# A scan kernel whose background work is moved to other chunks: new positions on four engines, and C's rows 56 bytes further on

## The reference, cut to what matters

```python
xz = x @ in_w.T + in_b
xm, res = jnp.split(xz, 2, axis=-1)
xc = conv_general_dilated(xm, conv_w)             # 4 taps, each channel by itself
xm = silu(xc + conv_b)
x_dbl = xm @ xp_w.T
delta = softplus(x_dbl[..., :64] @ dt_w.T + dt_b)
Bm, Cm = x_dbl[..., 64:80], x_dbl[..., 80:96]
A = -exp(A_log)

def step(h, ins):                                  # 512 channels x 16 states
    d_t, B_t, C_t, u_t = ins
    h = h * exp(d_t[:, :, None] * A) + (d_t * u_t)[:, :, None] * B_t[:, None, :]
    return h, einsum('bds,bs->bd', h, C_t)

y = (ys + xm * D_ssm) * silu(res)
return y @ out_w.T + out_b
```

## Time and profile before

| | us |
|---|---|
| median of 3 runs | 3793.13 (3785.04 to 3797.67) |
| profiled execution | 3805.45 |
| its span | 3804.0 |

### The profile page before, as it was taken

How to read it: one execution, slowest core, us unless ns; L and a number is a source line. 1 busy time by engine, 2 the same in 40 slices (tenths; PEclk the granted TensorE clock), 3 DMA queues, 4 the chain that set the end, 5 groups by cost and what they waited for, 6 DMA issues and landing times.

```text
span 3804.0 us, 45601 instructions
## 1 busy us (share of the span) xinstructions
PE 2862.1 (75%) x15274; PEld 2092.5 (55%) x15275; DVE 2344.1 (62%) x3190; ACT 1933.3 (51%) x3239; POOL 1890.0 (50%) x1807
## 2 busy tenths in 40 slices
PE   3787777787787987777777777777988179999930
PEld 2666556566565554565555665565565146666620
DVE  4877778778784434787777787785333123333338
ACT  4776777776673324767766867764223011111100
POOL 2777677677685010687766777776110510100042
PEclk8888999999899987889998999999998589999975
DMA  5010011011012010001100111111002111311022
GB/s 212 29 33 30 29 31 32 29 32 37 32 43 65 1 34 23 23 31 30 33 29 26 34 31 34 33 41 39 26 23 92 68 46 61 116 62 60 32 65 80
DMA packets 100973, 171.52 MB, mean 45 GB/s; under 512 B 14514, under 2 KB 52658, under 8 KB 100786
## 3 DMA queue, kind: packets, MB, share of 16 engines
q1 hardware_dynamic: 82066, 119.38, 9.9%
q0 software_dynamic: 15392, 47.99, 3.4%
q10 hardware_dynamic: 3328, 1.76, 0.2%
HBM read 126.75 MB, written 42.34 MB: 44 GB/s over the span
## 4 chain that ended last, share of the span: by engine, by line
PE 49%; DVE 21%; issue 12%; ACT 8%; POOL 8%; DMA 2%; SPq 0%; another core or an unknown queue 0%; DVEq 0%; POOLq 0%; ACTq 0%
PE psD L1056 16%; PE psD L1378 6%; PE psD L1152 6%; DVE arena L1580 6%; POOL arena L703 6%; PE psA L1172 4%; DVE arena L1528 3%; DVE arena L1561 2%; PE psD L1121 2%; PE psD L1255 2%; PE psA L1056 2%; PE psA L1230 2%; DVE arena L1565 2%; ACT arena L894 2%; ACT arena L904 1%
## 5 line engine op out<-in xcount | busy, mean ns | idle before, releaser
L703 POOL TENSOR_TENSOR arena<-arena 128x512 f32<-128x512 f32 x1024 | 1319.2, 1314 | 10.5 <-POOL carry L699 0.2
L1152 PE MATMUL psD<-ident,arena 128*128 128x128 f32 x4096 | 702.8, 298 | 450.2 <-DVE arena L1580 372.5
L1152 PEld LDWEIGHTS psD<-ident,arena 128*128 128x128 f32 x4096 | 493.4, 150 | 713.6 <-DVE arena L1580 425.4
L904 ACT ACTIVATE arena<-arena,negA 128x512 f32<-128x512 f32 x1024 | 717.0, 711 | 54.2 <-DVE arena L1580 53.8
L1580 DVE TENSOR_TENSOR_SCAN arena<-arena,carry,psD 128x512 f32<-128x512 f32 x512 | 637.5, 1269 | 150.1 <-PE psA L1172 136.4
L1580 DVE TENSOR_TENSOR_SCAN arena<-arena,psD 128x512 f32<-128x512 f32 x512 | 609.9, 1210 | 160.7 <-PE psA L1172 141.6
L1172 PE MATMUL psA<-ident,arena 128*128 128x128 f32 x4096 | 661.2, 287 | 9.5 <-POOL arena L703 9.5
L894 ACT ACTIVATE arena<-arena,bc 128x512 f32<-128x512 f32 x768 | 546.2, 712 | 174.9 <-PE psD L1152 174.6
L1172 PEld LDWEIGHTS psA<-ident,arena 128*128 128x128 f32 x4096 | 520.9, 150 | 13.1 <-POOL arena L703 13.1
L687 POOL TENSOR_SCALAR arena<-arena,bc 128x512 f32<-128x512 f32 x256 | 186.9, 730 | 536.5 <-PE psD L1152 519.8
L1056 PE MATMUL psD<-arena 128*128 128x512 f32 (+4 forms) x776 | 335.7, 568 | 45.4 <-POOL strip L647 30.5
(11 more groups left out here) (214 smaller groups left out, 3758.9 us busy)
## 6 DMA issues: line engine op xcount, KB each, us to landing
arena<-c_dram SPq DMA_DIRECT2D x256, 256.0 KB, 3.1
arena<-in_W POOLq DMA_DIRECT2D x16, 1024.0 KB, 7.6
xs_dram<-arena SPq DMA_DIRECT2D x20, 512.0 KB, 6.9
arena<-xs_dram SPq DMA_DIRECT2D x71, 128.0 KB
ys_dram<-arena POOLq DMA_DIRECT2D x70, 128.0 KB, 2.0
arena<-in_x SPq DMA_DIRECT2D x8, 1024.0 KB, 7.3
o_dram<-arena SPq DMA_DIRECT2D x32, 128.0 KB, 3.0
arena<-o_dram SPq DMA_DIRECT2D x4, 1024.0 KB, 5.6
```

Source lines behind the costliest of these rows:

```text
L703: pool.tensor_tensor(h_ring[:, c % H_SLOTS, :], h_ring[:, c % H_SLOTS, :], c_rows[:, v % C_SLOTS, :], ALU.mult).then_inc(c_weighed, 1)
L904: act.activation(da_ring[:, c % DA_SLOTS, :], dt[:, i % 2, f, :], ACT.Exp, scale=negA[:, f, n:n + 1]).then_inc(da_ready, 1)
L1152: mm = pe.transpose(psD[:, c % FILL_BANKS, j * P:(j + 1) * P], g[:, (c // KI) % 2, j, c % KI * P:(c % KI + 1) * P], ident[:, :])
```

## The change

The step numbers of most background work are replaced, TURN and MO run in steps 24 to 31 and no longer in 32 to 43, Z follows them, GATE runs in 38 to 44, IN is spread over every third step, SILU, XD and BCT come one or two steps later, the softplus of blocks 0 and 1 and of blocks 2 and 3 (two halves) keeps its order but stands nearly one operation to a step, and UT comes later. In STAGES and in PE's loop, TURN now stands ahead of Z. SP issues `store_c` and `keep_o2` three to two rows of C earlier. 14 unused words ahead of C's rows in the arena and 2 behind move C by 56 bytes, and what lies behind by 64.

```diff
-        WORDS = 41540
+        WORDS = 41552
...
+        carve(14)
         c_rows = by_ring(carve(4 * HALF))
+        carve(2)
         da_ring = by_ring(carve(6 * HALF))
...
-        IN = [7, 9, 11, 13]
-        SILU = 19
-        XD, BCT = [22], [24]
-        Z = [25, 27, 29, 31]
...
+        IN = [6, 9, 12, 15]
+        SQUARE = [8, 11, 14, 17]
+        SILU = 21
+        XD, BCT = [23], [25]
+        TURN, MO = [24, 25, 27, 29], [26, 27, 29, 31]
+        Z = [29, 31, 33, 35]
+        SLOPE, LOGS, RMS = [33, 35, 43, 44], 38, 40
...
+        REPLACE, FINISH, TIMES = [41, 42, 48, 50], [43, 44, 51, 52], [45, 46, 53, 54]
+        GATE = [38, 40, 42, 44]
+        UT = [47, 48, 55, 56]
...
-                    if n == 11 and q + 1 < ITEMS:
+                    if n == 8 and q + 1 < ITEMS:
                         store_c(i + 1)
-                    if n >= 12 and q - 1 >= 4:
-                        keep_o2(i - 1, n - 12)
+                    if q - 1 >= 4:
+                        for j in range(JT):
+                            if n == 8 + max(j, 1):
+                                keep_o2(i - 1, j)
...
+                    if k is not None and r in TURN:
+                        turn_y(i0 + k, TURN.index(r))
                     if p is not None and r in Z:
                         project_dt(i0 + p, Z.index(r))
-                    if k is not None and r in TURN:
-                        turn_y(i0 + k, TURN.index(r))
```

More of the change, by code:

```diff
@@ L380, in decoder_layer @@
         XNT = [3, 4]
-        SQUARE = [4, 5, 8, 9]
-        IN = [7, 9, 11, 13]
-        SILU = 19
-        XD, BCT = [22], [24]
-        Z = [25, 27, 29, 31]
-        SLOPE, LOGS, RMS = [33, 33, 40, 41], 34, 36
-        SMALL = [33, 34, 35, 36]
-        CUBIC = [35, 36, 42, 43]
-        SERIES = [37, 38, 44, 45]
-        REPLACE, FINISH, TIMES = [38, 39, 45, 46], [39, 40, 46, 47], [40, 41, 47, 48]
-        UT = [43, 44, 50, 51]
-        TURN = [32, 35, 38, 41]
-        MO = [34, 37, 40, 43]
-        GATE = [46, 48, 52, 54]
+        IN = [6, 9, 12, 15]
[5 more added lines that the diff above has]
+        SLOPE, LOGS, RMS = [33, 35, 43, 44], 38, 40
+        SMALL = [34, 36, 40, 46]
+        CUBIC = [35, 37, 45, 46]
+        SERIES = [38, 39, 47, 49]
+        REPLACE, FINISH, TIMES = [41, 42, 48, 50], [43, 44, 51, 52], [45, 46, 53, 54]
+        GATE = [38, 40, 42, 44]
+        UT = [47, 48, 55, 56]
         STAGES = (("mo", MO, -1, "dve", 1), ("xnT", XNT, 1, "act", 1), ("in", IN, 1, "dve", 4),
-                  ("xd", XD, 1, "act", 1), ("bcT", BCT, 1, "act", 1), ("z", Z, 1, "dve", 2), ("turn", TURN, -1, "dve", 1),
+                  ("xd", XD, 1, "act", 1), ("bcT", BCT, 1, "act", 1), ("turn", TURN, -1, "dve", 1), ("z", Z, 1, "dve", 2),
                   ("uT", UT, 1, "act", 1), ("gate", GATE, 0, "act", 1))
```

## The result

| | before | after |
|---|---|---|
| median, us | 3790.53 (4 runs, 3785.04 to 3797.67) | 3576.47 (4 runs, 3571.69 to 3576.84) |
| profiled execution | 3805.45 | 3571.69 |
| its span | 3804.0 | 3570.2 |

The ratio is 0.943, with a 95% interval of 0.941 to 0.945: 5.7% faster. The direction was forecast; the size was not.

A forecast was written before the change was run, and what follows sets the result against it. No engine is full; DVE and PE waiting for each other bound an item. Gaps falling from 28.0 to 17.3 us, less 1.0 for the port, save 9.7 a middle item, 130 together: 3663 us, forecast 3610 to 3735, range 3580 to 3800.

The forecast's parts named there:

- part 1: Silu block moved to step 21, covered by six scans; only a gap around xd stays: 7.5 us becomes 3.3.
- 2, leave: DVE's waits for the four leave products, now in steps 24 to 31 at PE's full clock: 8.85 us becomes 5.3.
- 3, z: Waits at the dt projections, moved to steps 29 to 35 with other DVE work ahead of the reader: 2.0 becomes 0.3.
- Part 4: Gate projections at steps 38 to 44 covered by DVE's work, Ln block at 38: 3.5 us becomes 2.0, between 0 and 4.
- 5, first projection: First input projection moved to step 6, behind open_y and ahead of the next fill: gap 1.15 us becomes 1.7.
- 5, open_y: Gap before scan 8, with the squares gone from steps 4 and 5: 5.0 us becomes 4.7 (4.4 to 5.0).
- Part 6: DVE operations and POOL shutting each other out of SBUF: +1.0 us an item, bounds -3.6 and +16.9.
- Part 7: C's rows offset by 56 bytes, the rest 64: no change to POOL's multiplication; at 1.25 us, 4 us gained in all.
- rival A: Each of 16 DVE operations an item waits a whole POOL operation: 87 us more, about 3880; chance 0.14.
- B: PE's clock falls to 1.2 GHz for xd and the four leaves, so a small gain: 3762 us; chance 0.15.
- D: The moves only pass the wait to the next link (open_y, xd, leave): within 0.3%; chance 0.07.
- C: Mo gaps halve, late ones vanish: 4.7 us more an item, about 3600; more if POOL's multiplication shortens; chance 0.14.

The follow-up runs named there:

- e6: The kernel before with only the Silu block one step later (SILU = 20 instead of 19): ratio 0.987 [0.986, 0.989].
- e2: The changed kernel without the offset words, so the new order with every tile where it was before: ratio 0.958 [0.955, 0.961], 3632 us.
- e13: The new order without the shift, POOL's product with C over 440 of 512 columns: ratio 0.947 [0.944, 0.950] to the kernel before.
- e14: The changed kernel with POOL's product with C over 384 of 512 columns: ratio 0.940 [0.937, 0.944] to the kernel before.
- e7: The changed kernel with only the gate projections put back to steps 46, 50, 53 and 57: ratio 0.9525 [0.949, 0.956] to the kernel before.
- e8: The changed kernel with open_y cut in four, one piece ahead of each of the first four additions: ratio 0.9413 [0.939, 0.944] to the kernel before.
- e9: The changed kernel with the xd product cut by blocks over steps 21, 22, 22 and 23: ratio 0.9425 [0.939, 0.947] to the kernel before.

## Why the prediction was right, and where it failed

The gaps of one middle item, in us:

| part | before | forecast | measured |
|---|---|---|---|
| 1, Silu block and xd | 7.5 | 3.3 | 3.53 |
| 2, leave | 8.85 | 5.3 | 5.03 |
| 3, z | 2.0 | 0.3 | 0.47 |
| 4, gate and Ln | 3.45 | 2.0 | 0.56 |
| 5, first projection | 1.15 | 1.7 | 1.39 |
| 5, open_y | 5.0 | 4.7 | 4.66 |
| sum | 28.0 | 17.3 | 15.6 |
| 6, the port, as DVE's busy time | 112.4 | +1.0 | -2.6 |

**Parts 1, 2, 3 and 5 held,** within about 0.3 us a row. e6 shows the reason of part 1 alone; for the others the rows agree with the reasons given, and no run takes them apart. The leaves came out at 1.23, 1.05, 1.80 and 0.95 where 1.2, 1.1, 1.8 and 1.2 were said. They were worked out from pitches (0.44 for a fill, 1.72 or 3.44 for a product) along the rows of the order.

**Part 7 failed, and it alone is enough to put the time outside the range.** The step was "at 1.25 the gain is 64 x 0.03 in each last item, 4 us in all", and "I take no change". Its lower bound was the shortest of 1024 products that all had their inputs at a distance of 0; that spread can't bound what another distance does. The product fell to 1.097. By its ratio the order alone takes 3632 us, and by the 40 us that the traces give to the shift some 3617; both are inside the range, and inside the forecast's own 3610 to 3735, and 3576 is not. "No row shows an offset other than multiples of 2048 bytes" was true of the rows chosen, but the trace of before held such a case: L725 and L728 above, 4.52 and 3.81 us for the same addition, one of them with its inputs 8 bytes apart.

**The second half of that step failed too:** that a shorter product would pay in the last items only, since these are "near POOL's 89 us". It is the other way round. POOL was taken as a share of a whole item (103 of 142.6 us, nobody's limit), but in the new order it works without a pause in the steps from 61 to 6 of the middle items and paces the others there (e2, e13, e14). The earlier trace rows showed DVE waiting for PE's addition, and the prediction stopped there; it didn't ask what PE's addition waits for. In the trace of before the answer was still small, 13.1 us in 15 waits; the new order made it 57.0 in 125. By the shift the last items gained 0.2 us in the old order and 1.1 in the new one, where the middle items gained 1.9 and the first 3.3.

**Part 4** was oversized by 1.4 us of remaining gap. 1.0 each had been put on the edges of the gate block and on the Ln block; one gap of 0.56 is left, and the Ln block (809.38 to 814.36) leaves none. e7 shows that the late steps cost a middle item 2.2 us, somewhat under half of it as gaps and the rest as longer busy times of DVE.

**Part 6** had the wrong sign. In the two scan phases DVE's busy time fell by 26.1 us, 22.0 of them by the order alone. DVE's operations beside POOL wait 7.4 us an item in all, not 9.2: replace costs 0.87 us on average (1.20 before) and the halo's 0.31 (0.51), while times u rose from 0.73 to 0.99. Of all L1568 and L1572 more than half still wait, but by 0.3 us on average, far from the 0.9 at which rival A would have decided. The order alone has 7.6, so this is hardly the shift's doing; why the operations meet POOL less often in their new steps was not tested. The Trainium skill (SBUF — State Buffer, Who interferes with whom) has a VectorE operation with two inputs in SBUF and a GpSimd operation that reads SBUF shut each other out. The medians well above the shortest (1050 against 657 ns) agree that they do; how often they meet is not in the rule, and the rule gave no size.

**First and last items.** 6 us were said for a first item, by the sum less leave, and 1 for a last one. The order alone gave 9.7 and 3.0. e6 names a part of both: the Silu block stands in the first and in the last items as well (2.8 and 1.9 us by one step), and that the last items were near POOL's busy time was no reason to leave them out: the order alone won 3.0 us there with the long product.

**Nothing elsewhere** was off by 8 us: the last leave of a group ends 24.4 us after the start of its last scan and not 28.3. This is part 7 again, not the order: with the order alone it ends 28.5 and 29.2 us after it, with the shift in the old order 25.8 and 25.6. A further 14 us of the spans' difference lie behind the last leave of the second group; what follows the last scan differs as much between chips (see above), so no run makes them the change's.

**The rivals.** A fell as told. B (leaves at the lower clock, 1.2 GHz) did not come: granted was 0.97 in the item, and all four leaves took 1.89 us. D, the wait that only moves on, fell with the order alone; e8 and e9 show it for two single gaps. C, put at about 3600 with a chance of 0.14, came nearest; but its reasons came in part only (mo gaps 5.03 of 8.85, late ones 0.56 of 3.45, all gaps 1.7 us an item better than forecast where C wanted 4.7), and its half sentence "if POOL's multiplication gets shorter by the offset, more" is what happened.

## What to carry to other kernels

When a wait's row names an engine, ask for what that engine itself was waiting: here DVE waited for PE, and PE for POOL, in stretches that busy shares over a whole item hide. A bound taken from the spread of durations holds for the conditions of the rows only. Before you set a term to nothing, look through the whole trace for the same operation under the new condition (here L728 beside L725); if there is none, a change of placement needs a run of its own. Gaps worked out from pitches along the printed order came within a few tenths of a microsecond. Two gaps that were cut to pieces moved and gave nothing back. And when two parts of a change are told apart, compare the stretches of the traces and not the medians alone.

## What the runs showed of the hardware

A GpSimd product of two float32 inputs in SBUF, 128x512, written over the first, takes 1.27 to 1.28 us when the inputs' starts differ by a multiple of 16 bytes, and 1.09 to 1.10 us at 4, 8, 12, 24, 40 and 56 bytes: some 14% less for a few unused words. An addition of 128x2048 takes 4.52 and 3.81 us (L725, L728).

The difference is one for each element. From 512 to 2048 elements the time grows by (4518 - 1276) / 1536 = 2.11 ns an element in the long case and by (3810 - 1092) / 1536 = 1.77 in the short one, and about 0.19 us don't grow in either. By these numbers, as an estimate, 440 columns take 1.12 us in the long case and 384 take 0.87 in the short one; e13 measured 1.122, e14 0.865.

The Trainium skill (GPSIMD Engine Reference, 3.1 Elementwise — side-by-side cycle accounting) gives an operation on two inputs about 2.6 cycles an element, and 4497 ns for an addition of 2048. At the 1.2 GHz of that page an estimate by the runs is 2.5 cycles in the long case and 2.1 in the short one. So the page agrees with the long case (4518 ns), which is the one that rows laid end to end get, and the runs show that less is possible.
